# Feed-forward probabilities turned two units behind their scores and ahead of the value products, with two of four phase barriers dropped

## Chip, cores and metric

One core of one Trainium2 chip runs the whole program; the other cores are idle. The metric is the device time of one execution in microseconds, from 3 timed executions of the kernel before (median, lowest, highest) and one more execution under the profiler.

## What is computed

The input is x of 8 sequences, 256 tokens each, 128 wide, in float32. Three layers follow each other, each on the layer norm of x: half a feed-forward block, a middle attention, half the same feed-forward block again.

```python
x = x + 0.5 * ffn(layernorm(x)); x = x + mid(layernorm(x)); x = x + 0.5 * ffn(layernorm(x))

def ffn(x):                       # 16 heads of 64, 4 key/value heads, window of 128, rotary, one sink per head
    h = rmsnorm(x, attn_norm_w)
    q, k, v = split(h @ qkv_w + qkv_b); q, k = rope(q), rope(k)
    x = x + (softmax_with_sink(q @ k.T / 8, causal and window) @ v) @ proj_w + proj_b
    h2 = rmsnorm(x, ffn_norm_w)
    topv, topi = top_k(h2 @ gate_w + gate_b, 4)          # 4 of 32 experts for each token
    return x + sum(softmax(topv)[e] * (silu(h2 @ Wg[e]) * (h2 @ Wu[e])) @ Wd[e] for e in topi)

def mid(x):                       # 16 heads: scores are the sum of 4 semantic and 4 rotary dimensions
    return softmax(scores with one null key, causal) @ v_with_null @ wo
```

## The kernel before

**Stages.** `program` runs five pieces on each engine: `attention(layers[0])`, `experts(0)`, `attention(layers[1])` (the middle), `attention(layers[2])`, `experts(1)`. Between them stands `phase`: the engine drains, counts up `phase_done`, and waits until all five engines have (L474 and L475). There are four such barriers.

**Units and frames.** An attention works on two sequences at a time (a round k of 4, that is 4 tiles lt of 128 queries). A round has 16 units s: tile lt = s // 4 and a group g = s % 4 of four heads. An even tile has 128 keys, an odd tile 256, in two halves. A frame is the place of one unit in the order of the program, and the 64 units of the four rounds follow each other. Each engine walks through the frames and does in each what is due there. On TensorE (`body`, L885 and after) a frame holds: the mask product of the new unit (`scores` half 0, L799), one front or tail step, the scores themselves (L807), `weigh` of the unit `lag + 1` behind (the value products, L869, L880 in the middle), `turn_probs` of the unit `lag` behind (transposes of the probabilities, L852), and the other front and tail steps. `lag` is 1 in a feed-forward and 2 in the middle. Front steps prepare the next sequence: `turn_x` (L737), `rope` (L747, L752), `value`, `null`. Tail steps finish a tile: `turn_r` (the reciprocals of the sums turned, L765), `project` (L773), `turn_h` (L777), `gate` (L780), `place` (L783 to L785); each is due at a number of units after the start of the round, `4 * lt + 6` for `turn_r` and so on (L229 to L236).

**Other engines in a frame.** VectorE takes the maxima of the scores (`row_max`: L1114, L1117), copies the turned probabilities of the first half of keys out of PSUM (`copy_pT`, L1122), makes the reciprocals (`normaliser`, L1133 and L1139), the rotary products (L1061), the residual (L1150), the gate's top four and the places of the rows (L1159 to L1186). ScalarE copies the value products out (`copy_y`, L1407), makes the exponentials (`exps`, L1385), and copies the second half of the turned probabilities (`copy_pT1`, L1396). With a lag above 1 that copy stands ahead of `exps`, with a lag of 1 behind it (that is in `body` already). SP stores the turned reciprocals in memory and loads them spread over all partitions (`store_rows`, `spread_rows`). POOL multiplies with them (`normalise`, L1639, output yT), scales rows (`rms_norm`), picks experts (`pick`) and sends rows off to the experts' regions in memory (`send`, four indirect DMAs for a tile, L1621). The first of the four sends of a tile also adds the tile's counts to `earlier` (L1618) and keeps `place_of` (L1619).

**Banks.** Four of the eight PSUM banks hold the scores (two units in turn), four are side banks for all else. `Layer.__init__` is a planner: it walks through the frames with estimated holding times (`HOLD_US`) and gives every use of a side bank the one that is free first (`bank_for`), and with it the semaphore by which its last owner frees it. The order in which it asks is the order of TensorE's program.

**Experts.** `experts` first makes a plan out of the counts in `earlier`: small products on TensorE (L911 to L919) and 14 small VectorE operations, up to the row numbers `rows_at` (L1288). POOL then waits for all rows sent (`sent0` to `sent3`) and for the plan, and gathers the first rows (L1713); SP loads the others. 24 groups of four blocks of 128 rows go through TensorE (L934 to L963). `find_answers` on VectorE works out where a token's answers lie.

## Time and profile before

| | us |
|---|---|
| median of 3 timed executions | 1419.59 |
| lowest, highest of them | 1399.04, 1426.07 |
| the profiled execution, its own time | 1410.39 |
| span of the profile, first to last instruction | 1408.6 |
| TensorE products busy in the span | 1004.7 (71%) |
| VectorE busy | 851.9 (60%) |
| POOL busy | 746.3 (53%) |
| ScalarE busy | 572.1 (41%) |
| mean granted clock of TensorE | 0.883 of 2.4 GHz |

The rows are all of the one profiled execution. A span of busy time is not always work: an instruction that is blocked counts as busy. In the views of waits, a wait is put down to what came last; "issue" means that nothing in the profile is seen to end it, which can also be a wait for several semaphores. The first feed-forward attention takes roughly the stretch up to 401 us, the first experts that up to 528, the middle up to 805, the second feed-forward attention up to 1186, the second experts the rest.

### The profile page before, as it was taken

What the parts mean: (1) busy time and instruction counts of PE and PEld (TensorE: products, weight loads), DVE (VectorE), ACT (ScalarE), POOL (GpSimd) and SP (SyncE); (2) the same over time, 40 slices, a digit from 0 to 9 for tenths busy, and PEclk for the clock granted to TensorE, in tenths of its full rate; (3) what the DMA queues carried; (4) which work ended last, traced back from release to release, by engine and by line L of the source; (5) the groups of instructions that cost most, each with busy time, mean ns of one, the idle gap of its engine ahead of it and who ended that gap; (6) DMA issues with size and microseconds to landing.
All of it is one profiled execution on the core that took longest, in us unless ns stands there. A gap on an engine that the chain in (4) does not pass through costs nothing.

```text
span 1408.6 us, 23364 instructions
## 1 busy us (share of the span) xinstructions
PE 1004.7 (71%) x6906; PEld 704.5 (50%) x6906; DVE 851.9 (60%) x2096; ACT 572.1 (41%) x2204; POOL 746.3 (53%) x940
## 2 busy tenths in 40 slices
PE   2888787888518892699899939888988882688300
PEld 2556555555416771355555526655656551577200
DVE  4778687886312433587777538888888761233121
ACT  0545454455304440355555605544545550244100
POOL 2235655655557404676665232457666557551475
PEclk9899999999758996799999969999999995799755
DMA  5686888777404421011111111334322211343221
GB/s 176 158 201 164 201 200 208 167 171 165 108 25 133 126 77 41 24 42 35 35 41 22 24 45 63 106 94 127 102 87 74 67 46 45 91 134 98 70 63 55
DMA packets 121816, 137.76 MB, mean 98 GB/s; under 512 B 16864, under 2 KB 96992, under 8 KB 121696
## 3 DMA queue, kind: packets, MB, share of 16 engines
q1 hardware_dynamic: 99728, 78.97, 19.6%
q10 hardware_dynamic: 10704, 34.21, 11.7%
q0 software_dynamic: 11264, 23.09, 5.8%
q8 instruction: 62, 1.02, 0.3%
q14 instruction: 58, 0.48, 0.1%
HBM read 57.24 MB, written 58.07 MB: 82 GB/s over the span
## 4 chain that ended last, share of the span: by engine, by line
PE 36%; DVE 15%; POOL 8%; issue 7%; POOLq 2%; DMA 2%; ACT 1%; DVEq 0%; SPq 0%; ACTq 0%
PE ps L944 6%; PE ps L852 4%; POOL shared L1723 4%; PE ps L834 4%; PE ps L963 4%; DVE top L1114 3%; PE ps L747 3%; PE ps L869 3%; DVE shift L1117 2%; DVE pT L1122 2%; POOLq L474 2%; PE ps L773 2%; PE ps L807 2%; PE ps L955 2%; PE ps L934 2%
## 5 line engine op out<-in xcount | busy, mean ns | idle before, releaser
L1385 ACT ACTIVATE prob<-ps,shift 128x128 f32<-128x128 f32 (+1 forms) x768 | 312.0, 420 | 211.5 <-DVE shift L1117 209.7
L1114 DVE TENSOR_REDUCE top<-ps 128x4 f32<-128x512 f32 (+1 forms) x192 | 182.4, 950 | 57.8 <-PE ps L807 27.5
L852 PE MATMUL ps<-tb,prob 128*128 128x128 f32 x1152 | 173.9, 288 | 0.0
L852 PEld LDWEIGHTS ps<-tb,prob 128*128 128x128 f32 x1152 | 126.8, 144 | 65.5 <-issue 63.1
L1122 DVE COPY pT<-ps 128x512 f32<-128x512 f32 x192 | 131.2, 683 | 46.9 <-PE ps L852 46.4
L1385 ACT ACTIVATION_READ_ACCUMULATOR prob<-ps,shift 128x1 f32 x768 | 157.4, 205 | 0.0
L869 PE MATMUL ps<-pT,v 128*64 128x256 f32 x768 | 116.4, 410 | 48.6 <-issue 17.7
L1639 POOL TENSOR_TENSOR yT<-yraw,spread 128x1024 f32<-128x1024 f32 (+1 forms) x48 | 82.4, 1717 | 121.0 <-DMA spread<-turned 91.6
L1621 POOL DMA_INDIRECT routed<-row_out,row_at x128 | 131.2, 1025 | 25.1 <-issue 24.0
L1713 POOL DMA_INDIRECT qT<-routed,rows_at x96 | 92.0, 958 | 72.7 <-PE ps L934 27.2
L807 PE MATMUL ps<-keyT,qT 64*128 64x256 f32 (+1 forms) x1024 | 124.7, 364 | 0.0
L1540 POOL TENSOR_TENSOR qT<-rot_a,swapped 128x512 f32<-128x512 f32 x64 | 81.1, 1269 | 66.6 <-issue 57.3
L1407 ACT ACTIVATE yraw<-ps 128x256 f32<-128x256 f32 x128 | 49.0, 383 | 153.8 <-PE ps L869 141.0
L747 PE MATMUL ps<-xT,wf 128*128 128x256 f32 x320 | 94.4, 428 | 19.7 <-DVE rot_a L1061 11.8
L807 PEld LDWEIGHTS ps<-keyT,qT 64*128 64x128 f32 x1024 | 81.6, 196 | 43.8 <-issue 38.7
L1304 DVE COPY prob<-ps 128x512 f32<-128x512 f32 x48 | 33.2, 691 | 116.3 <-PE ps L955 116.3
L834 PE MATMUL ps<-shared,qT 128*128 128x256 f32 (+1 forms) x256 | 102.7, 500 | 0.0
L773 PE MATMUL ps<-wf,yT 128*128 128x128 f32 x512 | 76.5, 313 | 31.6 <-POOL yT L1639 20.5
L869 PEld LDWEIGHTS ps<-pT,v 128*64 128x64 f32 x768 | 49.0, 140 | 89.6 <-issue 57.3
L1723 POOL DMA_INDIRECT shared<-answers,answer_at x64 | 61.7, 964 | 60.3 <-DMA answers<-yraw 41.1
L944 PE MATMUL ps<-shared,prob 128*128 x384 | 93.1, 386 | 0.0
L1645 POOL DMA_INDIRECT swapped<-answers,answer_at x64 | 62.7, 980 | 55.3 <-DMA answers<-yraw 41.5
(155 smaller groups left out, 1899.5 us busy)
## 6 DMA issues: line engine op xcount, KB each, us to landing
routed<-nothing ACTq DMA_DIRECT2D x16, 2048.0 KB, 12.9
swapped<-rot_b SPq DMA_DIRECT2D x160, 128.0 KB, 2.8
spread<-turned SPq DMA_DIRECT2D x64, 256.0 KB, 4.2
answers<-yraw SPq DMA_DIRECT2D x48, 256.0 KB, 2.3
shared<-in_w_up SPq DMA_DIRECT2D x32, 256.0 KB
qT<-routed SPq DMA_DIRECT2D x96, 64.0 KB, 2.0
shared<-in_w_down SPq DMA_DIRECT2D x32, 128.0 KB
routed<-row_out,row_at POOLq DMA_INDIRECT x128, 2.7
```

Source lines behind the costliest of these rows:

```text
L747: last = pe.matmul(misc[:, n * T:(n + 1) * T], w[:, 0:P], xT[:, :], start=True, stop=True)
L773: last = pe.matmul(misc[:, 0:D], yT[:, n * P:(n + 1) * P], w, start=(n == 0), stop=(n == blocks - 1))
L807: last = pe.matmul(ps[:, bank + side, T * n:T * n + keys(lt)], qT[rows, j, 2 * g + n, q0:q0 + P], keyT[rows, j, g // 2, 0:keys(lt)], start ...
L834: last = pe.matmul(to, q, heads, start=behind, stop=not behind and n == 1)
L852: last = pe.transpose(ps[:, BANK_SIDE + bank, h * P:(h + 1) * P], prob[:, s % 4, h, c * P:(c + 1) * P], ident)
L869: last = pe.matmul(y[DH * side:DH * side + DH, 0:2 * P], v[:, j, c, at:at + DH], pT[:, s % 2, c, 2 * P * side:2 * P * side + 2 * P], start ...
L944: last = pe.matmul(to, eT[:, g % 2, b, :], weights[:, bass.ds(at[b], 2 * DFF)], start=True, stop=True)
L1114: dve.tensor_reduce(top1[:, s % 2, :], score_view(L, s, lt), AX.X, ALU.max, negate=True)\
L1122: dve.tensor_copy(pT[:, s % 2, 0, :], ps[:, BANK_SIDE + L.turned[k, s][0][0], :]).then_inc(S["pT_ready"], 1)
L1385: last = act.activation(prob[:, s % 4, h, 0:keys(lt)], score_view(L, s, lt)[:, h, :], ACT.Exp, bias=shift[:, lt % 2, one:one + 1], accum_o ...
L1621: pool.indirect_dma_start(routed, bass.IndirectOffsetOnAxis(row_at[:, lt, n:n + 1], 0), row_out[:, lt, :], None).then_inc(S[f"sent{lt}"], 16)
L1723: pool.indirect_dma_start(last_answers[:, tile, n, :], None, answers, bass.IndirectOffsetOnAxis(answer_at[:, tile, n:n + 1], 0))\
```

## The change

It sets the lag of a feed-forward to 2. In all three attentions a frame's transposes come ahead of its value products, in the planner as on TensorE. In a feed-forward the last tile's normaliser (VectorE), `turn_r` (TensorE) and the DMAs behind it (SP) come one frame earlier. The barriers between an attention and its experts are dropped; TensorE then waits for the last `picked`, and VectorE's `find_answers` for the last `placed`. On POOL the counting moves out of `send` into `account`, and in the last round the four sends of tile 2 are held back to the frame of tile 3's `account`.

```diff
-        self.lag = lag = 1 if ffn else 2
+        self.lag = lag = 2
...
-            steps[4 * lt + 6].append((0, "turn_r", lt))
+            steps[4 * lt + (5 if ffn and lt == 3 else 6)].append((0, "turn_r", lt))
...
+            if frame.unit(lag):
+                k, s = frame.unit(lag)
+                self.turned[k, s] = [self.bank_for("turn_p0", ("pT_ready", UNITS * k + s + 1))]
+                if s // 4 % 2:
+                    self.turned[k, s].append(
+                        self.bank_for("turn_p1", ("pT1_ready", UNITS // 2 * k + 4 * (s // 8) + s % 4 + 1)))
             if frame.unit(lag + 1):
...
-            if frame.unit(lag):
...
         def program(eng, attention, experts):
             attention(layers[0])
+            experts(0)
             phase(eng, 0)
-            experts(0)
+            attention(layers[1])
             phase(eng, 1)
-            attention(layers[1])
-            phase(eng, 2)
             attention(layers[2])
-            phase(eng, 3)
             experts(1)
...
-                            for kk, lt in at_slot(frame, [4 * lt + 7 for lt in range(4)]):
+                            for kk, lt in at_slot(frame, [4 * lt + 6 + (lt < 3) for lt in range(4)]):
                                 spread_rows(kk, lt)
...
-                        for kk, lt in at_slot(frame, [4 * lt + 6 for lt in range(4)]):
+                        for kk, lt in at_slot(frame, [4 * lt + 5 + (lt < 3 or not L.ffn) for lt in range(4)]):
                             store_rows(kk, lt)
...
-                        if frame.unit(L.lag + 1):
-                            k, s = frame.unit(L.lag + 1)
-                            use = frame.weigh
-                            weigh(k, s, use)
                         if frame.unit(L.lag):
                             k, s = frame.unit(L.lag)
                             turn_probs(k, s)
+                        if frame.unit(L.lag + 1):
+                            weigh(*frame.unit(L.lag + 1), frame.weigh)
...
+                pe.wait_ge(*layers[2 * number].signals.at("picked", TILES))
                 pe.matmul(ps[0:E, BANK_XT, 0:NBLOCKS], earlier[:, :], mk[:, B_ONE:B_ONE + NBLOCKS],
...
-                        for kk, lt in at_slot(frame, (5, 9, 13, 17)):
+                        for kk, lt in at_slot(frame, (5, 9, 13, 16 if L.ffn else 17)):
                             normaliser(kk, lt)
...
+                        dve.wait_ge(*layers[2 * number].signals.at("placed", TILES))
...
+                def account(k, lt):
+
+                    tile = 4 * k + lt
+                    pool.wait_ge(*S.at("place_step", 3 * tile + 3))
+                    pool.wait_ge(*S.at("pick_ready", tile + 1))
+                    pool.wait_ge(*S.at("pick_step", 4 * tile + 4))
+                    pool.wait_ge(*S.at("h2_ready", tile + 1))
+                    if L is layers[0]:
+                        pool.wait_ge(blanked[lt], 16 * (k + 1))
+                    pool.tensor_tensor(earlier[:, :], earlier[:, :], picked[:, :], ALU.add).then_inc(S["picked"], 1)
...
+                            for kk, lt in at_slot(frame, [4 * lt + 17 for lt in range(4)]):
+                                account(kk, lt)
                             for n in range(TOPK):
                                 for kk, lt in at_slot(frame, [4 * lt + 17 + n for lt in range(4)]):
-                                    send(kk, lt, n)
+                                    if kk < ROUNDS - 1 or lt != 2:
+                                        send(kk, lt, n)
+                            for kk, lt in at_slot(frame, [UNITS + 13]):
+                                if kk == ROUNDS - 1:
+                                    for n in range(TOPK):
+                                        send(kk, 2, n)
```

TensorE in the first feed-forward, two units of which the second is the first of a new sequence. Before (L799 mask, L807 scores, L869 value products, L852 transposes, L737 turn_x, L747 rope):

```order
L799 MATMUL ps<-mk 128x512 x2
L737 MATMUL ps<-tb,hh 128x128 x2
L807 MATMUL ps<-keyT,qT 128x256 x4
L869 MATMUL ps<-pT,v 64x256 x4
L852 MATMUL ps<-tb,prob 128x128 x8
L799 MATMUL ps<-mk 128x2x128 x2
L747 MATMUL ps<-xT,wf 128x256 x2
L807 MATMUL ps<-keyT,qT 128x128 x4
L869 MATMUL ps<-pT,v 64x256 x4
```

Now, with line numbers three lower:

```order
L796 MATMUL ps<-mk 128x512 x2
L734 MATMUL ps<-tb,hh 128x128 x2
L804 MATMUL ps<-keyT,qT 128x256 x4
L849 MATMUL ps<-tb,prob 128x128 x8
L866 MATMUL ps<-pT,v 64x256 x4
L796 MATMUL ps<-mk 128x2x128 x2
L744 MATMUL ps<-xT,wf 128x256 x2
L804 MATMUL ps<-keyT,qT 128x128 x4
```

The transposes have moved ahead of the value products, and the value products are now the last work of the unit ahead of the next mask product and opening step.

ScalarE in the same attention, three units. Before (L1407 copy_y, L1385 exps, L1396 copy_pT1):

```order
L1407 ACTIVATE yraw<-ps 128x256
L1385 ACTIVATE prob,total<-ps,shift 128x256 x4
L1396 ACTIVATE pT<-ps 128x512
L1424 ACTIVATE junk,msq<-x 128x128
L1421 ACTIVATE rT<-ps 16x128
L1375 ACTIVATE xT<-ps,col 128x256
L1407 ACTIVATE yraw<-ps 128x256
L1385 ACTIVATE prob,total<-ps,shift 128x256 x4
L1396 ACTIVATE pT<-ps 128x512
```

Now:

```order
L1404 ACTIVATE yraw<-ps 128x256
L1393 ACTIVATE pT<-ps 128x512
L1382 ACTIVATE prob,total<-ps,shift 128x256 x4
L1421 ACTIVATE junk,msq<-x 128x128
L1418 ACTIVATE rT<-ps 16x128
L1372 ACTIVATE xT<-ps,col 128x256
L1404 ACTIVATE yraw<-ps 128x256
L1393 ACTIVATE pT<-ps 128x512
L1382 ACTIVATE prob,total<-ps,shift 128x256 x4
```

The copy of the turned probabilities stands ahead of the exponentials of the unit.

POOL at the end of a feed-forward attention, up to the first gather of the experts. Before (L1618 and L1619 the counting, L1621 sends, L1593 to L1605 pick):

```order
L1618 TENSOR_TENSOR earlier<-earlier,picked 128x32
L1619 COPY place_of<-place 128x4
L1621 DMA routed<-row_out,row_at 65664x128
L1593 TENSOR_TENSOR rsum<-esum,minus_one 128x1
L1596 TENSOR_TENSOR pairs<-picks 128x64
L1601 TENSOR_TENSOR picked<-pairs 128x32
L1603 COPY experts_of<-idxf 128x4
L1605 TENSOR_TENSOR wtop<-etop,rsum 128x4
L1621 DMA routed<-row_out,row_at 65664x128 x3
L1618 TENSOR_TENSOR earlier<-earlier,picked 128x32
L1619 COPY place_of<-place 128x4
L1621 DMA routed<-row_out,row_at 65664x128 x4
```

Now (L1614 and L1615 the counting, L1620 sends):

```order
L1614 TENSOR_TENSOR earlier<-earlier,picked 128x32
L1615 COPY place_of<-place 128x4
L1590 TENSOR_TENSOR rsum<-esum,minus_one 128x1
L1593 TENSOR_TENSOR pairs<-picks 128x64
L1598 TENSOR_TENSOR picked<-pairs 128x32
L1600 COPY experts_of<-idxf 128x4
L1602 TENSOR_TENSOR wtop<-etop,rsum 128x4
L1614 TENSOR_TENSOR earlier<-earlier,picked 128x32
L1615 COPY place_of<-place 128x4
L1620 DMA routed<-row_out,row_at 65664x128 x8
```

Four sends have moved from ahead of the last counting to behind it, so eight follow each other there.

## Rows read from the trace of the kernel before

**Rows 1.** Stretches (start:end us): busy us of each engine, clock, DMA share, GB/s

```profile
60.00:345.00 285.00, 235.87 (x1635) 160.15 (x1635) 221.39 (x530) 139.86 (x599) 159.88 (x226) 0.94 0.78 185
...
600.00:790.00 190.00, 173.13 (x1415) 110.57 (x1414) 147.37 (x385) 112.27 (x490) 118.01 (x124) 1.00 0.15 33
860.00:1140.00 280.00, 239.84 (x1727) 163.43 (x1725) 237.29 (x559) 149.87 (x638) 163.79 (x228) 0.97 0.31 90
```

**Rows 2.** TensorE's waits, 60 to 345 us: total us, times, longest

```profile
PE ps L869 <- issue: 8.0, 13, 1.6
...
PE ps L773 <- ACT yraw L1407: 7.3, 3, 3.3
PE ps L869 <- ACT pT L1396: 4.4, 2, 2.6
```

**Rows 3.** Timeline of ScalarE and TensorE about 370 us: start, duration, instruction

```profile
369.50 0.60 ACT L1396 ACTIVATE pT<-ps 128x512 f32<-128x512 f32 x1
...
370.20 1.08 PE L869 MATMUL ps<-pT,v 128*64 128x256 f32 x8 [1.75 <-issue]
371.22 1.09 PE L852 MATMUL ps<-tb,prob 128*128 128x128 f32 x8
```

**Rows 4.** Waits of TensorE and of its weight loads, 860 to 1140 us

```profile
PE ps L869 <- ACT pT L1396: 9.4, 4, 3.3
...
PE ps L869 <- issue: 5.3, 10, 1.4
PE ps L869 <- DVE pT L1122: 5.3, 4, 3.3
...
PEld ps L799 <- ACT prob L1385: 0.2, 1, 0.2
```

**Rows 5.** TensorE's waits in the middle, 600 to 790 us

```profile
PE ps L880 <- DVE pT L1122: 13.1, 13, 1.7
```

**Rows 6.** Chain of waits, 395 to 430 us: start, duration, what

```profile
403.24 11.96 POOLq L474
...
419.68 0.79 issue
```

**Rows 7.** Timeline from the first feed-forward to its experts

```profile
382.87 0.96 POOL L1621 DMA_INDIRECT routed<-row_out,row_at  x1 [0.30 <-issue]
...
386.84 2.33 POOL L1639 TENSOR_TENSOR yT<-yraw,spread 128x1024 f32<-128x1024 f32 x1 [3.02 <-DMA spread<-turned]
...
401.55 0.41 DVE L1186 CAST row_at<-place 128x4 uint32<-128x4 f32 x1
...
408.92 0.96 POOL L1621 DMA_INDIRECT routed<-row_out,row_at  x1 [0.30 <-issue]
...
415.24 0.26 PE L911 MATMUL ps<-mk,earlier 128*32 128x96 bf16 x1 [14.38 <-POOLq L474]
...
419.34 0.26 DVE L1288 TENSOR_SCALAR rows_at<-region_row,tb 128x96 uint32<-128x96 f32 x1
...
420.47 0.99 POOL L1713 DMA_INDIRECT qT<-routed,rows_at  x1 [10.58 <-DVE rows_at L1288]
```

**Rows 8.** Timeline from the second feed-forward to its experts

```profile
1167.73 0.97 POOL L1621 DMA_INDIRECT routed<-row_out,row_at  x1 [0.30 <-issue]
1172.09 2.33 POOL L1639 TENSOR_TENSOR yT<-yraw,spread 128x1024 f32<-128x1024 f32 x1 [3.39 <-DMA spread<-turned]
...
1186.72 0.40 DVE L1186 CAST row_at<-place 128x4 uint32<-128x4 f32 x1
...
1205.59 0.98 POOL L1713 DMA_INDIRECT qT<-routed,rows_at  x1 [10.54 <-DVE rows_at L1288]
```

**Rows 9.** The seven sends issued from 400 to 412 us (line L1621)

```profile
DMA to landing us min/median/max: 2.2/2.2/2.3
```

**Rows 10.** VectorE's shift L1117, 90 to 345 us: its group, and its durations in ns

```profile
L1117 DVE TENSOR_TENSOR shift<-top,neg_sink 128x4 f32<-128x4 f32 x46 | 25.9, 562 | 1.6
...
L1117 DVE TENSOR_TENSOR shift<-top,neg_sink x46: 161/163/2203, 93.1 to 343.4; 128x4 f32<-128x4 f32 x46
```

More of the change, by code:

```diff
@@ L469, in build @@
         ENGINES = 5
-        PHASES = ("ffn0", "experts0", "mid", "ffn1", "experts1")
         def phase(eng, n):
```

18 lines of the change are left out of this document (2 added, 16 removed).

## The prediction

> **What bounds the kernel now.** I read the table of stretches first. In both feed-forward attention stretches and in the middle one TensorE is the busiest engine: 235.87 of 285 us, 173.13 of 190 and 239.84 of 280 [rows 1]. VectorE is hard behind it, 237.29 of 280 in the second feed-forward. So a feed-forward unit (64 units in about 335 us, 5.2 us each) is not held by one engine; TensorE and VectorE hand a bank back and forth, and each has some 15% of idle time. The idle time of TensorE, read in the view of waits, is what a change of order can win. In the first feed-forward stretch the value products (L869) waited 8.0 us for "issue" and 4.4 for ScalarE's pT copy, and the projection (L773) waited 7.3 for ScalarE's yraw copy [rows 2]. The "issue" is the pT copy as well, as one piece of the timeline shows: ScalarE's copy starts at 369.50 and takes 0.60, and the products start at 370.20, 0.10 after its end [rows 3]. In the second stretch L869 waited 9.4 + 5.3 + 5.3 us [rows 4], in the middle L880 waited 13.1 us for pT [rows 5]. These products stand one unit behind their transposes and ahead of the next transposes, so nothing but the scores lies between a transpose, its eviction, and its use.
>
> The second place is where a feed-forward attention gives way to its experts. TensorE stands still there. The chain of waits has 11.96 us of POOL's drain in it [rows 6], and the rows before and after it say why: the last row is sent off at 408.92, the first gather of rows starts at 420.47 [rows 7]. Between them lie the drain, the barrier, and then the plan (L911 to L1288), each after the other. The second time is alike [rows 8].
>
> **The barrier, part by part.** Removed: two of four barriers. Now TensorE starts the plan as soon as the 16th picked is in, that is when account(3, 3) is done; VectorE's plan runs while POOL still sends. What POOL's first gather then waits for is its own sends' landing. Added and moved for it: the four sends of tile 2 of the last round go behind account(3, 3), so that 8 sends follow it, not 4; and tile 3's normaliser and turn come one unit earlier.
>
> First feed-forward, against its own rows [rows 7]. (a) Tile 3. Its yT starts at 386.84 because the spread row landed late (idle 3.02 before it), while POOL was free at 382.87 + 0.96 = 383.83. With turn_r(3) a unit earlier, ahead of project(2), its DMAs are issued about 5 us sooner and the wait is gone: what is late next is POOL's own queue. But yT(2) comes later too: turn_r(2)'s copy on ScalarE stands behind exps, which now start behind the pT copy and one transpose more; I take 0.9 us. So 3.0 - 0.9 = 2.1 us. (b) The last row_at ended at 401.55 + 0.41 = 401.96; now 399.9. account takes 0.5, and a send every 0.96 + 0.30 = 1.26: the last of 8 starts at 400.4 + 7 x 1.26 + 0.1 = 409.3. (c) A send lands 2.2 us after its issue [rows 9], so 411.5; the gather follows what releases it by 0.79 [rows 6], rounded up to 1.0 for four semaphores: 412.5 against 420.47, **8.0 us**. The plan took 415.24 to 419.60 = 4.4 us; started at 400.4 it is over at 404.8 and hidden. Second feed-forward [rows 8]: POOL free at 1167.73 + 0.97 = 1168.70, yT at 1172.09, so 3.4 - 0.9 = 2.5 us; row_at at 1187.12 - 2.5 = 1184.6, last send 1194.0, gather 1197.3 against 1205.59, **8.3 us**. Together 16.3.
>
> Bound from below: after the last send's instruction (ended 409.88) the drain still took until 415.20, 5.3 us. If that is the time until rows are really down, the gather can't start before 409.3 + 0.96 + 5.3 = 415.6, and the gain is 4.9 and 5.2, 10.1 in all. I take the 2.2 of the landing row, since that measures it.
> The Trainium skill (DMA: Bandwidth & Descriptors, "Two DMAs through the same engine are not ordered") says that the completion semaphore is what tells that the data has landed. By that rule the drain adds nothing that the four sent semaphores don't give, and the sum is 16.3; by the drain's own row it would be 10.1. No row of before tells the two apart.
>
> Where the cover goes: if VectorE or POOL were not free at account(3, 3), the plan's 4.4 us would come back only past 411.5, a slack of 6.7 us. The middle's barrier in and out stays.
>
> **The lag.** In the feed-forward a unit's probabilities are turned two units behind the scores and ahead of the value products of the unit before, no longer one behind and after them. No instruction is added: same transposes, same copies. Four things move. (1) Between a transpose and the products that use it now lie the older products, the rest of the unit, the next scores and the next transpose. The last is new, 1.09 us for two key halves [rows 3]. (2) ScalarE's pT copy goes ahead of exps (the code does that for a lag of two), so it no longer waits for the newest maxima; the ACT rows of the change show it. (3) yraw is written a unit later, so ScalarE's wait for an old yT, behind which the projection's 7.3 us lie, has a unit more. (4) The planner deals the four side banks anew. Here a wait is put in: the front step that opens a unit finds its bank last held by the value products just ahead of it, in 21 of 64 units per feed-forward by the plan's own rules, 9 before. It must sit out their eviction with only the mask product as cover, which I put at 0.2 us each, 4 us per feed-forward; against that stand the openings that waited for the pT copy of the transpose just ahead, which are gone with the same order of size. I count the two as nothing, bound 0 to 8 us of loss in all.
>
> What can be won at most: 8.0 + 4.4 + 7.3 = 19.7 in the first, 9.4 + 5.3 + 5.3 = 20.0 in the second [rows 2, 4]; 39.7 in all. At least: nothing, if every wait only moves to the next hand-over. I take **half, 19.9 us**, nearer to neither, for VectorE: with 20 us less in 280 its 237.29 busy us would fill 91%, and its own waits can't all go. Also 20 of the 64 first transposes get the bank of the transpose before them, and wait for its copy themselves (15 before).
> A rule that speaks against the change: some of VectorE's busy time is really blocking. Its small shift (L1117, 128x4) takes 161 ns at best and 562 ns in the mean, 46 times in a stretch of 255 us [rows 10], 18 us of blocking in it.
> The Trainium skill (SBUF — State Buffer, "Who interferes with whom") says that a VectorE instruction with two SBUF inputs and a GpSimd instruction that reads SBUF shut each other out for a whole instruction. The long ones here lie beside POOL's work, which agrees. By that rule a denser unit keeps all of this blocking, which lets VectorE take back what TensorE gives: the gain of the lag would be nearer 0 than 39.7.
>
> **The middle.** Only the order of transposes and products changes, and its banks. Its products waited 13.1 us in 190 [rows 5]; a transpose of up to 1.09 us [rows 3] now stands ahead of them and covers most of a mean wait of 1.0. But in 20 of 64 units that transpose's own bank is freed by the very copy that the products waited for, and there the wait only moves to it; and six projections now get the bank that the y copy has just to leave, about 0.5 us each. So 13.1 x 0.6 = 7.9, less 3, rounded down for VectorE: **4 us**, bounds -3 and 13.
>
> **Sum.** The profiled execution took 1410.4 us around a span of 1408.6. 1410.4 - 16.3 - 19.9 - 4 = 1370.2. The three timed runs had a median of 1419.6 and went from 1399.0 to 1426.1; the profiled one lies below their median, and the four average 1413.8, 3.4 above it. I add 3.8 for that: **1374 us**. Ends: everything won 1410.4 - 16.3 - 39.7 - 13 = 1341; low gains only 1410.4 - 10.1 + 8 + 3 = 1411.
>
> **Rivals.** A: the barrier alone counts. For it: TensorE and VectorE both near 86% in the second feed-forward, so that a wait taken from one turns up at the other. Against it: the pT waits come from order, with ScalarE half idle. Time: 1410.4 - 16.3 + 3.8 = 1398, with the drain's bound 1404. Chance 0.32.
> B: slower, through ScalarE. Its exps of a unit now start behind this unit's transpose, the products, the y copy and the pT copy. The products and the y copy stood there before; new are 1.09 + 0.60 = 1.7 us in the 64 feed-forward units of two key halves [rows 3], 109 us in all. Exps free the score banks, so from the point at which they end after TensorE has come to the unit two later, each of these us is on the path. Against it: TensorE waited for exps once, 0.2 us [rows 4], and two units are 10 us, of which exps would take 1.7 more. It would take half of the 109 to make the kernel 1410.4 - 16.3 + 54 = 1448. Chance 0.06.
> C: as A, with the landing of rows late as in the drain and the new bank waits in full, no gain beyond noise: 1411. Inside A's chance.
> The forecast, with the lag winning a third or more, has 0.62. A measurement of this kernel tells about 2% from no change, that is 28 us: faster needs 1391 or less, which is the forecast (0.62); within 2% is A and C (0.32); slower 0.06. The range, 1346 to 1408, leaves out the tip of the full gain, the worst of C, and B.
>
> **What would show it.** Right: no drain row between the last send and the first gather, the plan's L911 (now L907) under the sends, gathers starting 3 to 4 us after the last send's issue; TensorE's waits of the value products for pT down from 20 us to under 5 per stretch; the feed-forward stretches some 10 us shorter each; ScalarE's pT copies ahead of exps. Wrong: gathers starting 6 us or more behind the last send; L852's successor or the openings (L747, L737) waiting as long as L869 did; TensorE waiting at the mask product for exps, which is B; an unchanged middle stretch with VectorE over 90% busy.

## The result, and the profile after

| | before | after |
|---|---|---|
| median of the timed executions, us | 1422.83 (4) | 1452.18 (4) |
| lowest, highest | 1399.04, 1426.69 | 1446.40, 1459.82 |
| the profiled execution, its own time | 1410.39 | 1446.40 |
| span | 1408.6 | 1444.6 |
| ratio after / before, 95% interval | | 1.0307 (1.0156 to 1.0459) |

The change makes the kernel slower, by 3.1% with 1.6 to 4.6% as the interval. 1374 was forecast and 1452 measured, far above the upper end of 1408. The profiled execution of the kernel before is none of its four timed ones; that of the kernel after is the fastest of its four. The ratios here and below leave out executions in a slower state, those more than 1.5% above the fastest of their kernel (one of the kernel before, in the group of e5 to e8, took 5246.78 us), so a ratio need not be that of the two medians.

To see where the time went I read the timelines for a few landmarks and subtract. A scores' stretch runs from the first score product of an attention (L807, now L804) to the start of its last group of them, an exit from there to the first gather of the experts (L1713, now L1719).

| us | first ffn scores | exit | middle scores | second ffn scores | exit |
|---|---|---|---|---|---|
| before | 327.1 (38.0 to 365.1) | 55.4 | 241.4 | 302.9 (847.3 to 1150.2) | 55.4 |
| after | 358.5 (37.6 to 396.1) | 46.5 | 235.6 | 336.4 (862.2 to 1198.6) | 46.2 |
| difference | +31.4 | -8.9 | -5.8 | +33.5 | -9.2 |

These sum to +41.0. The rest (start, experts, hand-overs of the middle) is 5.0 shorter together, which gives the 36.0 between the two profiled executions. So the exits and the middle came out near their forecasts, and the feed-forward scores' stretches lost 65 us where they were to win 20.

**The stretches.** The view of stretches of the kernel after, with the columns of [rows 1]: start:end and length, then busy us of TensorE, its weight loads, VectorE, ScalarE, POOL, then clock, DMA share, GB/s. The first two lines are stretches of the same place in the program as those of before, the last two the whole scores' stretches.

```profile
60.00:345.00 285.00, 224.39 (x1453) 148.11 (x1453) 202.65 (x487) 122.84 (x533) 138.25 (x193) 0.89 0.70 167
...
885.00:1165.00 280.00, 225.09 (x1493) 146.71 (x1493) 208.78 (x495) 127.61 (x550) 146.98 (x203) 0.91 0.29 83
...
37.60:396.10 358.50, 282.78 (x1850) 186.20 (x1849) 250.26 (x601) 158.14 (x688) 177.42 (x246) 0.89 0.70 167
862.20:1198.60 336.40, 275.60 (x1850) 179.45 (x1849) 253.24 (x601) 158.60 (x688) 176.20 (x246) 0.92 0.27 78
```

And the same whole stretches of the kernel before, for comparison:

```profile
38.00:365.10 327.10, 271.92 (x1866) 184.15 (x1865) 252.18 (x602) 161.39 (x695) 176.33 (x246) 0.93 0.77 183
847.30:1150.20 302.90, 260.26 (x1866) 177.50 (x1865) 257.17 (x602) 162.30 (x695) 176.09 (x245) 0.97 0.29 87
```

In the short windows every engine does less in the same time, not only one: nobody became the bound. In the whole stretches VectorE, ScalarE and POOL have the busy time that they had, to 4 us. TensorE is idle 358.5 - 282.8 = 75.7 us where it was idle 55.2, and 60.8 where it was 42.6: some 20 us more each time. The other 11 and 15 us are the same products at a lower granted clock: 271.92 x 0.93 = 253 and 282.78 x 0.89 = 252. (The clock is the mean of the stretch as a share of 2.4 GHz.) A TensorE that stands still more often also has the lower clock here; which of them comes first, these rows don't say.

**TensorE's waits**, where [rows 2] and [rows 4] had theirs. First feed-forward, 60 to 380 us (who waited for whom: total us, times, longest):

```profile
PE ps L770 <- DVE pT L1118: 29.7, 6, 7.8
PE ps L780 <- DVE pT L1118: 9.5, 5, 2.0
PE ps L774 <- DVE pT L1118: 7.2, 5, 3.3
PE ps L777 <- DVE pT L1118: 6.6, 3, 2.6
PE ps L762 <- DVE pT L1118: 5.3, 1, 5.3
PE ps L749 <- DVE pT L1118: 4.4, 5, 2.3
```

Second feed-forward, 885 to 1165 us:

```profile
PE ps L780 <- DVE pT L1118: 20.5, 5, 4.6
PE ps L774 <- DVE pT L1118: 14.2, 5, 2.9
PE ps L770 <- DVE pT L1118: 7.8, 6, 1.5
PE ps L749 <- DVE pT L1118: 4.0, 3, 3.6
PE ps L777 <- DVE pT L1118: 3.7, 4, 1.6
PE ps L744 <- DVE pT L1118: 2.4, 1, 2.4
PE ps L762 <- DVE pT L1118: 1.9, 1, 1.9
PE ps L849 <- ACT prob L1382: 1.1, 2, 0.6
```

The value products' wait for pT (L869, now L866), 12.4 and 20.0 us in [rows 2, 4], is gone from both lists. Five other lines took its place: L770 `project`, L774 `turn_h`, L777 `gate`, L780 `place`, L762 `turn_r`, all tail steps. They sum to 58.3 and 48.1 us. None of them reads pT. They wait for VectorE's copy of pT because it frees the **bank** that they are to write.

The whole stretches can be added up. All waits of TensorE listed from 37.6 to 396.1 us come to 75.6, all of its idle time but 0.1; from 38.0 to 365.1 us in the kernel before they come to 54.8 of 55.2. Waits for a bank that VectorE's copy of pT frees (tail steps, and L744 and L749, the openings) are 64.5 of the 75.6, and were 4.2 of the 54.8. All others fell from 50.6 to 11.1. In the second stretches the bank waits went from 4.4 to 54.5 and the others from 37.9 to 6.2. So the reorder removed more waits than the prediction had listed, and put in more still.

One such wait, in the timeline of TensorE, VectorE, ScalarE and POOL (start, duration, instruction, in brackets the idle time before it):

```profile
1006.15 0.65 PE L866 MATMUL ps<-pT,v 128*64 128x256 f32 x4
1006.67 1.22 DVE L1110 TENSOR_REDUCE top<-ps 128x4 f32<-128x1024 f32 x1
...
1006.74 0.33 PE L774 MATMUL ps<-tb,row_out 128*128 128x128 f32 x1
...
1006.85 0.38 ACT L1404 ACTIVATE yraw<-ps 128x256 f32<-128x256 f32 x1 [1.25 <-PE ps L866]
1007.33 2.33 POOL L1638 TENSOR_TENSOR yT<-yraw,spread 128x1024 f32<-128x1024 f32 x1 [2.15 <-DMA spread<-turned]
1007.92 1.76 DVE L1113 TENSOR_TENSOR shift<-top,neg_sink 128x4 f32<-128x4 f32 x1
...
1009.61 0.86 DVE L1057 SCALAR_TENSOR_TENSOR rot_a<-ps,bias_col,tb 128x256 f32<-128x256 f32 x2
...
1010.89 0.69 DVE L1118 COPY pT<-ps 128x512 f32<-128x512 f32 x1
...
1011.63 0.21 PE L780 MATMUL ps<-picked,mk 128*128 128x32 bf16 x1 [4.57 <-DVE pT L1118]
```

The unit's transposes were over by 1006.23 (L849 at 1005.60, 0.63 long). Their copy on VectorE starts at 1010.89, because the maxima, a shift that takes 1.76 us (161 ns at best in [rows 10]), a rotary product and the norm's statistics stand in VectorE's queue ahead of it. TensorE stands for 4.57 us with a product of 0.21 us at the head of its queue, and the next unit's scores, which have their banks, stand behind it. The value products' bank was copied out by ScalarE from 1006.85 to 1007.23, 3.7 us before VectorE even began its copy. In the kernel before, 29 of the 80 tail steps of a feed-forward got that bank, by the plan's rules.

**Middle.** The waits of TensorE from 600 to 790 us, where [rows 5] had 13.1 us in 13 waits, the longest 1.7:

```profile
PE ps L877 <- DVE pT L1118: 10.5, 7, 5.5
PE ps L770 <- ACT yraw L1407: 2.4, 6, 0.4
PE ps L849 <- DVE pT L1118: 1.1, 4, 0.6
```

One wait of 5.5 us at the start of the middle makes half of the 10.5. The kernel before has such a wait too, but ahead of 600 us. So the whole stretches are to be compared, and there the line of the kernel before is

```profile
PE ps L880 <- DVE pT L1122: 20.5, 14, 7.4
```

and the one after 10.5 as above: 10.0 us less. The two new waits that were forecast are there, 2.4 us for the y copy (six, as counted) and 1.1 us for the transpose's bank. The stretch is 5.8 us shorter.

**The exit**, where the chain in [rows 6] had 11.96 us of drain. The chain of waits from 425 to 450 us (start, duration, what), with the last send but one, the last send's landing (counted from its issue) and the first gather:

```profile
438.12 0.96 POOL routed L1620
439.08 0.30 issue
439.38 2.23 DMA routed<-row_out,row_at
...
441.82 0.79 issue
442.61 0.98 POOL qT L1719
```

And POOL's timeline at the second exit, answering to [rows 8]:

```profile
1241.56 0.96 POOL L1620 DMA_INDIRECT routed<-row_out,row_at  x1 [0.30 <-issue]
1244.76 0.98 POOL L1719 DMA_INDIRECT qT<-routed,rows_at  x1 [2.24 <-DMA routed<-row_out,row_at]
```

A gather follows the issue of the last send by 3.2 us. The plan's first product (L907) runs at 430.2 under the sends and is not in the chain.

### The profile page after: what moved, and what is told of

Read it like the earlier page. It is cut to its first block, busy times and chain, and to the rows that moved or that the text cites. A ratio compares the mean times of both kernels' runs of the same rounds, so it can differ in the third digit from the quotient of the medians.

```text
span 1444.6 us, 23358 instructions
## 1 busy us (share of the span) xinstructions
PE 1037.2 (72%) x6906; PEld 714.8 (49%) x6906; DVE 850.2 (59%) x2096; ACT 566.6 (39%) x2204; POOL 745.7 (52%) x940
## 4 chain that ended last, share of the span: by engine, by line
PE 35%; DVE 16%; POOL 9%; issue 7%; DMA 2%; ACT 1%; POOLq 1%; DVEq 0%; SPq 0%; ACTq 0%
PE ps L940 6%; PE ps L831 4%; POOL shared L1729 4%; PE ps L959 4%; DVE top L1110 3%; PE ps L744 3%; PE ps L770 3%; PE ps L849 3%; PE ps L804 2%; DVE shift L1113 2%; DVE pT L1118 2%; PE ps L951 2%; PE ps L866 2%; PE ps L930 1%; POOL routed L1620 1%
## 5 line engine op out<-in xcount | busy, mean ns | idle before, releaser
L849 PE MATMUL ps<-tb,prob 128*128 128x128 f32 x1152 | 171.9, 287 | 4.9 <-ACT prob L1382 3.4
L1382 ACT ACTIVATION_READ_ACCUMULATOR prob<-ps,shift 128x1 f32 x768 | 162.0, 211 | 0.0
L849 PEld LDWEIGHTS ps<-tb,prob 128*128 128x128 f32 x1152 | 131.5, 145 | 54.5 <-issue 33.0
L1620 POOL DMA_INDIRECT routed<-row_out,row_at x128 | 131.1, 1025 | 25.6 <-issue 24.7
L804 PE MATMUL ps<-keyT,qT 64*128 64x256 f32 (+1 forms) x1024 | 133.7, 385 | 0.0
L1118 DVE COPY pT<-ps 128x512 f32<-128x512 f32 x192 | 130.9, 682 | 4.5 <-PE ps L849 4.3
L770 PE MATMUL ps<-wf,yT 128*128 128x128 f32 x512 | 82.2, 327 | 60.6 <-DVE pT L1118 40.1
L1719 POOL DMA_INDIRECT qT<-routed,rows_at x96 | 91.0, 948 | 56.4 <-PE ps L930 28.1
L866 PE MATMUL ps<-pT,v 128*64 128x256 f32 x768 | 112.6, 400 | 1.6 <-DVE gl L1155 0.9
L770 PEld LDWEIGHTS ps<-wf,yT 128*128 128x128 f32 x512 | 75.6, 234 | 72.6 <-DVE pT L1118 45.9
L804 PEld LDWEIGHTS ps<-keyT,qT 64*128 64x128 f32 x1024 | 87.1, 208 | 48.3 <-issue 40.1
L831 PE MATMUL ps<-shared,qT 128*128 128x256 f32 (+1 forms) x256 | 105.6, 513 | 0.5 <-ACT prob L1382 0.2
L1057 DVE SCALAR_TENSOR_TENSOR rot_b<-ps,bias_col,tb 128x256 f32<-128x256 f32 x160 | 69.5, 476 | 48.4 <-PE ps L744 48.0
L744 PE MATMUL ps<-xT,wf 128*128 128x256 f32 x320 | 91.7, 418 | 7.5 <-DVE pT L1118 4.2
```

What stands on the lines that cost most here:

```text
L744: last = pe.matmul(misc[:, n * T:(n + 1) * T], w[:, 0:P], xT[:, :], start=True, stop=True)
L770: last = pe.matmul(misc[:, 0:D], yT[:, n * P:(n + 1) * P], w, start=(n == 0), stop=(n == blocks - 1))
L804: last = pe.matmul(ps[:, bank + side, T * n:T * n + keys(lt)], qT[rows, j, 2 * g + n, q0:q0 + P], keyT[rows, j, g // 2, 0:keys(lt)], start ...
L831: last = pe.matmul(to, q, heads, start=behind, stop=not behind and n == 1)
L849: last = pe.transpose(ps[:, BANK_SIDE + bank, h * P:(h + 1) * P], prob[:, s % 4, h, c * P:(c + 1) * P], ident)
L866: last = pe.matmul(y[DH * side:DH * side + DH, 0:2 * P], v[:, j, c, at:at + DH], pT[:, s % 2, c, 2 * P * side:2 * P * side + 2 * P], start ...
```

## The experiments

The theories when the first four were written: (1) tail steps wait for banks that VectorE's late copy frees; (2) the lag itself costs, with `exps` behind one more copy; (3) transposes ahead of value products cost by themselves. Landmarks of each are in the table behind the last experiment. e1 to e4, e5 to e8 and e9 to e11 are three groups of runs, each with its own runs of the kernel before (medians 1408.28, 1408.43, 1410.1); the change itself was measured in a fourth.

**e1_tail.** Lag and order as before, barriers dropped and tile 3 early as in the change.

```diff
-        self.lag = lag = 2
+        self.lag = lag = 1 if ffn else 2
...
-                        if frame.unit(L.lag):
+                        if frame.unit(L.lag) and not (True):
                             k, s = frame.unit(L.lag)
                             turn_probs(k, s)
                         if frame.unit(L.lag + 1):
                             weigh(*frame.unit(L.lag + 1), frame.weigh)
+                        if frame.unit(L.lag) and (True):
+                            k, s = frame.unit(L.lag)
+                            turn_probs(k, s)
```

(and the same order in the planner)

> Everything of the change but its order and its lag: two barriers dropped, counting and sends moved, tile 3 one unit earlier; the feed-forward keeps a lag of 1 and all three attentions keep the value products first. All theories: from the last scores of a feed-forward to the first gather 46 to 48 us (55.4 before), the scores' stretches as before (327 and 303 us, within 5), the middle 241 us. Total 17 to 20 us below the kernel before, about 1395 to 1403.

Measured: 1402.45 against 1408.28, ratio 0.9964 (0.9909 to 1.0019). The total, the middle (242.1) and the exits (45.7 and 46.6) came within 1.1 us of what was expected. The stretches did not come back within the 5 us that were expected: 344.7 and 310.4, against 327.1 and 302.9. What makes the first of them so long stands below, under "One wait in the first feed-forward". The total says that the loss of the change sits in lag, order and what follows from them.

**e2_hold.** The change as it is, but the planner's estimate of how long the copy of a feed-forward's first transpose keeps its bank is 3.0 us, not 1.5, so it deals that bank later.

```diff
-               turn_p0=(0.65, 1.5), turn_p1=(0.65, 4.0), turn_r=(0.4, 2.5), project=(2.0, 1.0), turn_h=(0.4, 2.0),
+               turn_p0=(0.65, 1.5), ffn_p0=(0.65, 3.0), turn_p1=(0.65, 4.0), turn_r=(0.4, 2.5), project=(2.0, 1.0), turn_h=(0.4, 2.0),
...
-                self.turned[k, s] = [self.bank_for("turn_p0", ("pT_ready", UNITS * k + s + 1))]
+                self.turned[k, s] = [self.bank_for("ffn_p0" if ffn else "turn_p0", ("pT_ready", UNITS * k + s + 1))]
```

> The change with one number of the planner's table changed, for the feed-forwards only: a bank with turned probabilities counts as held 3.0 us after the transposes, not 1.5. Order and lag stay as changed. By the plan's rules no tail step then gets a bank that VectorE's copy of the same unit's transposes frees (25 did); 22 get the bank of the value products just ahead, freed by ScalarE. Theory 1 (the slow-down is TensorE waiting at tail steps for VectorE's pT copy, through the banks dealt): the feed-forward stretches fall from 358 and 336 us to 305 to 330 each, waits of tail steps for pT from 58 and 48 us to under 10, total 1375 to 1405. Theory 2 (exps late behind the copies, or the lag itself) and theory 3 (transposes ahead of products whatever the banks): stretches stay at 345 or more, total 1430 to 1450.

Measured: 1406.9, ratio 1.0003 (0.9952 to 1.0054): 45 us less than the change by the medians, 33 by the two profiled executions. The total is 2 us above what theory 1 had expected, and only one of the two stretches fell as it had expected. The program has the same instructions in the same order; a number in the planner alone moved the banks. The second feed-forward fell from 336.4 to 304.1, and its waits of TensorE (885 to 1140 us) are

```profile
PE ps L777 <- DVE rot_a L1057: 10.2, 5, 2.5
PE ps L749 <- DVE rot_a L1057: 8.4, 4, 3.0
PE ps L770 <- DVE v L1088: 5.9, 3, 3.2
```

without any tail step waiting for pT. The first feed-forward stayed at 355.2. No tail step waits for pT there either, but five projections wait 30.7 us (60 to 345 us), where in the change five had waited 26.5 for pT:

```profile
PE ps L770 <- DVE v L1088: 30.7, 5, 7.0
```

`project` there got the bank of a `value` step. Its timeline at 188 to 200 us shows a chain through three engines:

```profile
188.88 1.30 SPq L643 DMA_DIRECT2D spread<-turned  x2
...
194.15 2.33 POOL L1638 TENSOR_TENSOR yT<-yraw,spread 128x1024 f32<-128x1024 f32 x1 [4.27 <-DMA spread<-turned]
...
196.44 1.05 POOL L1567 TENSOR_TENSOR rstd<-powers,minus_half 128x4 f32<-128x4 f32 x1
...
197.53 1.54 DVE L1040 TENSOR_SCALAR xn<-xr,mv,rstd 128x128 f32<-128x128 f32 x2 [5.30 <-POOL rstd L1567]
...
199.88 0.36 DVE L1088 TENSOR_TENSOR v<-ps,row 128x256 f32<-128x256 f32 x1
```

The root of the norm stands behind POOL's yT, yT waits for the spread rows, VectorE waits for the root, and the value copy that frees the bank stands behind VectorE's wait. It is the same fault, a bank in the hands of an engine that is late, with another owner. So the owner of the bank decides, and dealing it to someone else need not help.

**e3_ffn_products_first.** Lag 2 stays, the feed-forward's value products go ahead of the transposes again, in the planner and on TensorE; the middle and all else as in the change.

> The change with the value products ahead of the transposes again in the feed-forwards, in plan and program; the lag stays 2 and the middle stays as changed. Tail steps then get the bank of the same unit's value products 27 times, of transposes never. Theory 1 and theory 3: stretches 300 to 330 us each, total 1375 to 1405. Theory 2 (the lag): 345 or more, total 1430 or more.

Measured: 1390.5, ratio 0.9863 (0.9777 to 0.995); stretches 335.6 and 299.3. The total is in the range of theories 1 and 3; the first stretch is 6 us above theirs, and holds a long wait that is shown below. The lag of 2 by itself shows no cost, and no gain beyond the scatter either.

**e4_lag1_turn_first.** The opposite half: `self.lag = lag = 1 if ffn else 2`, transposes first everywhere.

> The change with the feed-forward's lag at 1 again, transposes still ahead of the products. By the plan's rules 29 tail steps get the bank of the same unit's transposes. Theory 1: as slow as the change or slower, stretches 350 us or more, total 1440 to 1480 (with a lag of 1 ScalarE's copy stands behind exps as well). Theory 2: the lag was the cost, stretches about 327 and 303, total about 1400. Theory 3: slow as in theory 1.

Measured: 1447.24, ratio 1.0274 (1.0169 to 1.038); stretches 358.2 and 335.3, those of the change to 1.1 us. Its waits of TensorE from 60 to 380 us begin with `PE ps L770 <- DVE pT L1118: 24.4, 6, 6.0`. The order alone makes the loss, and the lag has no part in it. Theory 2 falls.

**e5_barrier_only.** e1 with tile 3's `turn_r`, store, spread and normaliser at their old units.

```diff
-            steps[4 * lt + (5 if ffn and lt == 3 else 6)].append((0, "turn_r", lt))
+            steps[4 * lt + 6].append((0, "turn_r", lt))
...
-                        for kk, lt in at_slot(frame, (5, 9, 13, 16 if L.ffn else 17)):
+                        for kk, lt in at_slot(frame, (5, 9, 13, 17)):
```

> As e1_tail, but tile 3 comes at its old unit as well: only the barriers, the counting and the sends differ from the kernel before. If moving tile 3 costs time inside the attentions (theory: it re-deals the banks with a lag of 1), the scores' stretches go back to 327 and 303 us and the exits take 48 to 49 us, total about 13 to 15 us below before and 0 to 10 below e1_tail. If e1_tail's long stretches (345 and 310) were scatter of one execution, this kernel is 1 to 3 us slower than e1_tail.

Measured: 1392.0 against 1408.43, ratio 0.9922 (0.9874 to 0.997). Between the medians it is 16.4 us. The early tile 3 shows no gain in the total here; e1, which has it, stood 10 us higher in another group of runs against a kernel before that was the same to 0.2 us, and the ten times of each overlap (1383.76 to 1415.05 and 1377.65 to 1402.6).

**e6_lag2_products_first_late3.** e3 with the late tile 3 of e5.

> As e3_ffn_products_first, but tile 3 at its old unit. If the early tile 3 helps only at the exit: stretches as in e3 (336 and 299), exits 47 to 48 instead of 45, total 3 to 6 us above e3. If it costs inside: 5 to 15 us below e3.

Measured: 1393.43, ratio 0.9944 (0.9895 to 0.9992), 2.9 above e3. Its exits are 49.8 and 47.1 against 45.1 and 45.0: with the lag of 2 the early tile 3 does shorten the exit, by 4.7 and 2.1 us. Against e5 (1392.0, the same with a lag of 1) the lag of 2 makes 1.4 us: no difference.

**e7_barrier_mid_order.** e5 with transposes first in the middle alone.

> As e5_barrier_only, with the middle's transposes ahead of its products (as in the change); feed-forwards as before. The middle 236 us instead of 241, all else as e5: 5 to 7 us below e5.

Measured: 1396.5 (1362.65 to 1410.93), a scatter that gives no ratio, so the 5 to 7 us below e5 can't be told from the total. Its profile is clear on the point in question: the middle takes 235.9 us where e5's took 242.0. There the order wins 6 us by itself.

**e8_scalar_copies.** The change, banks and order and all, with one edit: in a feed-forward ScalarE makes the first half's copy of pT, behind `copy_y` and ahead of `copy_pT1` and `exps`. The same banks are dealt to the same steps; only the engine that frees them is another.

```diff
-                        if frame.unit(L.lag):
+                        if frame.unit(L.lag) and not L.ffn:
                             k, s = frame.unit(L.lag)
                             copy_pT(k, s)
...
+                def copy_pT0(k, s):
+                    act.wait_ge(*S.at("pT_full", UNITS * k + s + 1))
+                    act.activation(pT[:, s % 2, 0, :], ps[:, BANK_SIDE + L.turned[k, s][0][0], :], ACT.Copy).then_inc(S["pT_ready"], 1)
...
+                        if frame.unit(L.lag) and L.ffn:
+                            copy_pT0(*frame.unit(L.lag))
```

> The change as it is, banks dealt as in the change, but in the feed-forwards ScalarE makes the copy of the first half of the turned probabilities too, behind the copy of the products and ahead of the exps; VectorE makes none. Theory 1 (tail steps wait for VectorE's queue through their bank): the bank is free within some 1.3 us of the transposes; tail-step waits for it fall to under 10 us per stretch, stretches 300 to 335 us, total 1370 to 1410. Theories 2 and 3: no better than the change, or slower, since exps start another 0.6 us later in every unit: 1440 or more.

Measured: 1375.12, ratio 0.9794 (0.9718 to 0.9871): 77 us less than the change. The waits of TensorE, 885 to 1100 us:

```profile
PE ps L770 <- ACT pT L1397: 6.0, 6, 1.1
PE ps L774 <- ACT pT L1397: 4.9, 5, 1.0
PE ps L777 <- ACT pT L1397: 4.9, 5, 1.0
PE ps L780 <- ACT pT L1397: 3.6, 5, 0.7
```

The same four steps wait for the same banks as in the change, but 1.1 us at most where it was up to 4.6. In all it is 19.4 us there, more than the 10 that were expected. This is the direct test of the cause: the wait in the change is VectorE's queue ahead of the copy. It also refutes theory 2 once more, since `exps` now stand behind yet another copy.

The edit does a second thing: it takes the copies off VectorE, whose busy time in the two stretches falls from 250.3 and 253.2 to 215.5 and 220.2 us. e9, the next experiment, tells the two apart.

**e9_scalar_copies_products_first.** e8 with the order of e3.

> As e8_scalar_copies (ScalarE makes both copies of turned probabilities in the feed-forwards), with the value products ahead of the transposes there, in plan and program. If transposes first is of use by itself once the bank is freed soon (my theory): products wait for pT again, 10 to 20 us per stretch, stretches 3 to 10 us longer than in e8 (330 and 297), total 1380 to 1395. If transposes first still costs something (rival): stretches 5 us or more shorter than in e8, total under 1370.

Measured: 1367.41, ratio 0.9723 (0.9633 to 0.9812), the fastest of all. Stretches 321.9 and 292.3, 8.4 and 5.1 below e8's. The four lines above are gone; the largest wait from 885 to 1100 us is now

```profile
PE ps L755 <- DVE rot_a L1066: 12.4, 5, 3.8
```

Together with the change, e3 and e8 this makes a table of four (first and second stretch, us):

| | VectorE copies | ScalarE copies | difference |
|---|---|---|---|
| transposes first | 358.5, 336.4 (the change) | 330.3, 297.4 (e8) | -28.2, -39.0 |
| products first | 335.6, 299.3 (e3) | 321.9, 292.3 (e9) | -13.7, -7.0 |

With the products first no tail step waits for the copied bank, and taking the same copies off VectorE brings 20.7 us, 11.7 of them one wait that is shown in the next paragraph; with the transposes first it brings 67.2. So VectorE's lighter load can't be the whole of what e8 gained.

The total came under the 1370 that had been set for the rival, which is that the order still costs something with ScalarE's copy. By the stretches it is not shown: the 8.4 us are less than the difference of that one wait, and the 5.1 lie within the scatter of the second stretch. In the totals, e10 below, which has e8's order and banks, ran in the same group as e9, and its four times (1375.74 to 1385.33) lie above e9's four (1365.3 to 1374.55).

**One wait in the first feed-forward.** In the profiled executions of e1, e2, e3, e7, e8 and e10, and not in the others, one projection of the last round waits 15.9 to 17.2 us for POOL's yT, which itself waits over 19 us for its spread rows. In e8:

```profile
357.73 2.33 POOL L1644 TENSOR_TENSOR yT<-yraw,spread 128x1024 f32<-128x1024 f32 x1 [19.23 <-DMA spread<-turned]
360.21 3.75 PE L770 MATMUL ps<-wf,yT 128*128 128x128 f32 x16 [16.72 <-POOL yT L1644]
```

and the same place in e9:

```profile
349.04 2.33 POOL L1653 TENSOR_TENSOR yT<-yraw,spread 128x1024 f32<-128x1024 f32 x1 [9.44 <-DMA spread<-turned]
351.52 3.75 PE L776 MATMUL ps<-wf,yT 128*128 128x128 f32 x16 [5.50 <-POOL yT L1653]
```

In the change the longest wait of this kind is 7.5 us. e5 and e7 have the same program up to there, and only e7 has the long wait. So it is no property of a kernel's order, it accounts for most of the spread in the first column of the table below, and it makes the first stretches of e8 and e2 longer, not shorter. What makes the rows late is not known.

**e10_scalar_copies_root_first** and **e11_products_first_root_first.** e8 and e3 with POOL's root of a norm ahead of its yT, after the chain found in e2.

```diff
+                        for b, par in norms_at(L, f, -3, 2):
+                            root(b)
                         for kk, lt in at_slot(frame, [4 * lt + 9 for lt in range(4)]):
                             normalise(kk, lt)
-                        for b, par in norms_at(L, f, -3, 2):
-                            root(b)
```

> As e8_scalar_copies, with POOL's reciprocal root of a sequence (rstd) ahead of the yT product that falls into the same unit, in the feed-forwards. Theory: the first feed-forward stays at 330 us while the second goes to 297 because yT waits there for the spread rows (32.5 us in all) and the root stands behind it, so that VectorE waits 21.4 us for the root. Then that wait falls under 8 us, the first stretch to 310 to 322, the second to 292 to 297, total 1355 to 1370. Rival: the DMAs of the first stretch (78% share) hold it by the swapped and spread rows themselves; stretch stays at 328 to 332, total 1372 to 1378.

> As e3_ffn_products_first (335.6 and 299.3 us, VectorE makes the first copies), with the root ahead of yT. By the theory of e10 VectorE's wait for the root, 24.2 us in the first stretch, falls under 8, the stretch to 315 to 325, total 1370 to 1382. By its rival nothing moves: 1388 to 1392.

Measured: e10 1378.55, ratio 0.9793 (0.9702 to 0.9885), no gain on e8; its rival's figures (a first stretch of 328 to 332) came, not the theory's. VectorE's wait for the root (60 to 345 us) fell from 21.4 to 6.8 us, and its wait for the projection rose from 8.3 to 15.5: the time moved on. e11 1374.43, ratio 0.9789 (0.9686 to 0.9891); the same wait fell from 24.2 to 8.8 and the first stretch from 335.6 to 321.9. But e3 has the long wait of the last paragraph (17.2 us) and e11 has not (6.6), which is most of those 13.7 us, and e9 has the 321.9 too, with 28.4 us of waiting for the root. So no gain of the root's order is shown. What bounds the first feed-forward at 322 us is left open; POOL's yT still waits for SP's spread rows there (25.4 us in e9, 15.5 in e11, 34.6 before, from 60 to 345 us).

| | first ffn | exit | middle | second ffn | exit | median | ratio |
|---|---|---|---|---|---|---|---|
| e1_tail | 344.7 | 45.7 | 242.1 | 310.4 | 46.6 | 1402.45 | 0.9964 |
| e2_hold | 355.2 | 45.9 | 236.6 | 304.1 | 45.9 | 1406.9 | 1.0003 |
| e3_ffn_products_first | 335.6 | 45.1 | 236.0 | 299.3 | 45.0 | 1390.5 | 0.9863 |
| e4_lag1_turn_first | 358.2 | 46.4 | 236.5 | 335.3 | 46.3 | 1447.24 | 1.0274 |
| e5_barrier_only | 326.8 | 45.7 | 242.0 | 310.9 | 48.4 | 1392.0 | 0.9922 |
| e6_lag2_products_first_late3 | 328.0 | 49.8 | 235.9 | 303.9 | 47.1 | 1393.43 | 0.9944 |
| e7_barrier_mid_order | 341.0 | 45.9 | 235.9 | 306.4 | 45.8 | 1396.5 | |
| e8_scalar_copies | 330.3 | 45.7 | 235.1 | 297.4 | 46.0 | 1375.12 | 0.9794 |
| e9_scalar_copies_products_first | 321.9 | 45.5 | 236.0 | 292.3 | 45.5 | 1367.41 | 0.9723 |
| e10_scalar_copies_root_first | 329.7 | 46.2 | 235.9 | 297.0 | 45.9 | 1378.55 | 0.9793 |
| e11_products_first_root_first | 321.9 | 45.4 | 236.5 | 295.1 | 45.1 | 1374.43 | 0.9789 |

The landmarks are those of each kernel's profiled execution. The first feed-forward of the kernels with a lag of 1 and the old order (before, e1, e5, e7) lies between 326.8 and 344.7 though little in it differs, so differences under 18 us in that column say nothing; the second lies between 302.9 and 310.9, so there differences under 8 us say nothing.

## Why the prediction was wrong

**The barrier: right.** 8.0 and 8.3 us were forecast, 8.9 and 9.2 came. What counted was the landing: the gather starts 3.2 us behind the last send's issue, 2.23 for the landing (2.2 in [rows 9]) and 1.0 more to its start. The lower bound from the drain's row, 10.1 in all, did not hold. The Trainium skill's rule (DMA: Bandwidth & Descriptors, "Two DMAs through the same engine are not ordered") is that the completion semaphore tells that the data has landed. The trace agrees: behind the semaphores alone the gather starts 1.0 us after the landing (441.61, then 442.61). With neither lag nor order changed, e5 measured barriers and sends together as 0.8% (0.3 to 1.3), that is 11 us, where 16.3 had been forecast with tile 3's part in it.

**The middle: right.** 4 us forecast, 5.8 measured, and 6.1 between e7 and e5. In the whole stretch the products' wait for pT fell by 10.0 us, where 7.9 was forecast (from a window that missed its longest wait, 7.4), and the two counter-costs, 3 us in the forecast, are 3.5 in the waits.

**The lag: wrong, and this is the step.** "I take half, 19.9 us" became -31.4 and -33.5. The 39.7 us of waits that it was half of did go; what failed is item (4), "The planner deals the four side banks anew", and in it "I count the two as nothing, bound 0 to 8 us of loss in all." That item priced the openings alone. By the plan's own rules, counted in the same way, 29 tail steps of a feed-forward had the bank of the same unit's value products in the kernel before and none that of the same unit's transposes; after the change none has the former and 25 the latter. The tail steps cost 58.3 and 48.1 us in some 20 waits each, and they had no price, because the question asked of each bank was "how far ahead is its last owner" and not "which engine frees it, and what stands in that engine's queue". In the rows at 1006 us the bank that ScalarE frees is back 0.4 us after the product's end (1006.80 to 1007.23), the one that VectorE frees 5.4 us after the transposes' (1006.23 to 1011.58); the longest wait for the latter was 7.8 us.

On the openings the sum was near and the mechanism was not. L749 and L744 waited 6.2 us in the first stretch and 6.4 in the second, where 4 were put; but all of it is for VectorE's copy of pT, and no wait of an opening for the value products' copy is listed, which was the wait that had the price. The prediction also said that openings behind the transpose just ahead "are gone". By the plan 10 front steps that open a unit had such a bank before and 12 have it after, and these waits (L737 and L747 before, 4.2 and 4.4 us) grew.

The shown cause has two parts. That the order of transposes and products makes the loss is shown by e1, e3 and e4 (both orders with both lags), and that it acts through the banks by e2 (the same instructions with other banks), clearly in the second stretch only. That the lateness of VectorE's copy sets the size of it is shown by e8 beside e3 and e9. The lag of 2 is innocent: e3, e6.

The bound "at least nothing, if every wait only moves to the next hand-over" was the second fault. A wait that moves need not keep its length: the waits for the bank of VectorE's copy grew from 4.2 and 4.4 us in the two stretches to 64.5 and 54.5, and all others fell by less, from 50.6 and 37.9 to 11.1 and 6.2. A small slip beside it: 3.8 us were added where the four executions lie 3.4 above the profiled one.

**Rival B** (slower through ScalarE's `exps`, 1448) gave nearly the time measured, by luck, since its mechanism was another: `L849 <- ACT prob` is 1.1 us in the second stretch, and e8, which loads ScalarE more, is faster. **The argument from blocking** on VectorE was sound and too weak. The Trainium skill (SBUF — State Buffer, "Who interferes with whom") says that a VectorE instruction with two SBUF inputs and a GpSimd instruction that reads SBUF contend, and that the loser blocks. The 1.76 us shift at 1007.92, which ends with POOL's yT (1009.68 and 1009.66), agrees; but the argument bounded the gain at zero, while such a shift, now ahead of a copy that frees TensorE's bank, was 1.6 us of a loss of 4.57. **Rival A** (the barrier alone, 1398) is what e1 built, 1402.45, and e5 without the early tile 3, 1392.0.

## What to carry to other kernels

When a change alters the order in which PSUM banks are dealt, list for every use who frees the bank it gets, on which engine, and what that engine has in its queue ahead of the freeing instruction; price all uses, not only those near the edit. Short steps with a bank of their own to write are the dangerous ones, since a product of 0.2 us that waits 4.6 us stops everything behind it. If the order is wanted, move the freeing copy to an engine with a short queue: ScalarE here, busy 158 of the 358 us in the change (e8, 0.9794 of the kernel before and not 1.0307). With the value products first in the feed-forwards as well (e9) it is 0.9723.

And look for a single long wait before two stretches are compared: here one of 16 to 17 us was there in e7 and not in e5, whose code is the same up to there.

## What the runs showed that was not expected

- One number in the planner's estimate of a holding time (1.5 to 3.0 us) was worth 45 us by the medians, 3% of the kernel, with no instruction moved (e2_hold against the change).
- POOL's drain lasted 5.3 us beyond its last send's instruction in the kernel before, while rows land 2.2 us after their issue; semaphores alone let the gather start 3.2 us after the issue. What the drain does in the rest is not known.
- TensorE's mean granted clock was 0.89 and 0.92 of 2.4 GHz in the change's feed-forward stretches, against 0.93 and 0.97, with the engine idle about 20 us longer in each. But e9 had 0.91 from 60 to 345 us with TensorE busy 245.9 of 285, and was the fastest, so the clock alone ranks nothing here.
- The early tile 3 went with 10 us more at a lag of 1 (e1 against e5, in different groups of runs) and shortened the exits at a lag of 2 (e3 against e6). Why is not settled.
